# Second feed-forward layer from two 12-bit halves of the gelu in one-pass float32r, with a new table of work places

## Time and profile before

| | |
|---|---|
| median of 3 runs | 1874.81 us (1872.44 to 1875.64) |
| span of the profiled execution | 1875.9 us |
| its own time | not listed apart from the runs; the median lies 1.1 us under the span |
| TensorE clock granted, mean | 0.967 |
| PE busy | 94% of the span |
| DVE busy | 75% |
| ACT busy | 63% |
| POOL busy | 54% |

### The profile page before, as it was taken

One profiled execution on the slowest core, in us unless ns is written; L12 is line 12 of the kernel. 1 busy time (PEld: TensorE's weight loads), 2 busy tenths in 40 slices (PEclk: granted clock), 3 DMA queues, 4 the chain that ended last, 5 costly groups with the idle time before them and its releaser, 6 DMA issues.

```text
span 1875.9 us, 74519 instructions
## 1 busy us (share of the span) xinstructions
PE 1757.2 (94%) x29935; PEld 1283.4 (68%) x29935; DVE 1413.3 (75%) x2997; ACT 1173.6 (63%) x2795; POOL 1020.8 (54%) x3192
## 2 busy tenths in 40 slices
PE   6879899999999999999999999999999999999875
PEld 4545567777777777777777777777777777777653
DVE  4656767787778877787778877787778777787454
ACT  3445666666666666666666666666666666666521
POOL 2102245666566666666566666666566656666632
PEclk8889999999999999999999999999999999999965
DMA  8511111111111111111111111111111111111000
GB/s 228 162 30 37 38 45 40 42 47 48 45 43 43 51 45 45 39 50 45 45 43 46 50 45 42 42 51 45 45 41 48 48 45 45 41 48 29 20 22 21
DMA packets 140912, 92.94 MB, mean 50 GB/s; under 512 B 20196, under 2 KB 139800, under 8 KB 140568
## 3 DMA queue, kind: packets, MB, share of 16 engines
q1 hardware_dynamic: 136368, 87.91, 17.2%
q10 hardware_dynamic: 4200, 0.27, 0.2%
HBM read 31.50 MB, written 18.35 MB: 27 GB/s over the span
## 4 chain that ended last, share of the span: by engine, by line
PE 57%; DVE 19%; SPq 7%; issue 6%; DMA 4%; POOL 3%; ACT 3%; DVEq 0%; ACTq 0%; POOLq 0%
PE gen_bank L766 10%; PE gen_bank L868 9%; PE value_bank L729 8%; DVE nmax L1121 8%; PE score_bank L697 7%; PE max_banks L559 6%; SPq L414 5%; DMA lowstage<-qpiece 3%; PE gate_bank L761 2%; DVE stats L1242 2%; DVE qaug L1137 2%; PE gen_bank L581 2%; PE gen_bank L807 2%; PE gen_bank L776 2%; SPq L417 2%
## 5 line engine op out<-in xcount | busy, mean ns | idle before, releaser
L1068 ACT ACTIVATE probs<-score_bank 128x512 f32<-128x512 f32 x1024 | 604.2, 600 | 238.8 <-PE score_bank L697 226.0
L1121 DVE TENSOR_REDUCE nmax<-max_banks 128x2 f32<-128x1024 f32 x512 | 622.6, 1216 | 89.5 <-PE max_banks L561 85.5
L697 PE MATMUL score_bank<-qaug,kaug 98*128 98x512 bf16 x1024 | 370.9, 387 | 2.4 <-ACT probs L1068 1.4
L729 PE MATMUL value_bank<-probs,vaug 128*32 128x128 f32 x8192 | 332.6, 280 | 0.0
L729 PEld LDWEIGHTS value_bank<-probs,vaug 128*32 128x32 f32 x8192 | 193.9, 109 | 123.2 <-issue 93.6
L1656 POOL TENSOR_TENSOR diff<-gates 128x16 f32<-128x16 f32 x472 | 126.3, 267 | 235.1 <-ACT gates L1074 233.8
L766 PE MATMUL gen_bank<-w2T,hT 128*128 128x256 f32 x1024 | 252.1, 389 | 0.0
L559 PE MATMUL max_banks<-kaug,qaug 64*128 64x512 bf16 x512 | 199.9, 390 | 37.4 <-DVE nmax L1121 35.1
L766 PEld LDWEIGHTS gen_bank<-w2T,hT 128*128 128x128 f32 x1024 | 184.3, 190 | 33.7 <-issue 13.8
L561 PE MATMUL max_banks<-kaug,qlow 64*128 64x512 bf16 x512 | 200.8, 392 | 0.0
L868 PE MATMUL gen_bank<-x1piece,w1Tb 128*128 128x128 bf16 x3072 | 195.2, 220 | 0.5 <-DVE x1rest L1396 0.5
(11 more groups left out here) (233 smaller groups left out, 2968.2 us busy)
## 6 DMA issues: line engine op xcount, KB each, us to landing
qstage<-qpiece SPq DMA_DIRECT2D x384, 64.0 KB
lowstage<-qpiece SPq DMA_DIRECT2D x192, 64.0 KB
xt<-in_L_attn_x SPq DMA_DIRECT2D x64, 128.0 KB
xk<-in_L_attn_x SPq DMA_DIRECT2D x16, 512.0 KB, 7.4
residual<-x2s SPq DMA_DIRECT2D x64, 128.0 KB
x2f<-residual SPq DMA_DIRECT2D x64, 128.0 KB
out<-x SPq DMA_DIRECT2D x64, 128.0 KB
raw<-in_L_ffn_W SPq DMA_DIRECT2D x2, 1024.0 KB, 8.3
```

Of the source, the lines that this page charges most:

```text
L697: pe.matmul(score_bank[t % 2][:, :], kaug[0:AUG, r, tt, u, :], qaug[:, r, u, :, :].rearrange("p h s -> p (h s)"), start=True, stop=True).t ...
L729: last = pe.matmul(value_bank[32 * g:32 * g + 32, :].rearrange("p (k t) -> p k t", k=HG)[:, :, uv * BLOCK_POS:(uv + 1) * BLOCK_POS], vaug[ ...
L1068: act.activation(probs[:, t % 4, :], score_bank[t % 2][:, :], ACT.Exp).then_inc(exp_done, 1)
L1121: dve.tensor_reduce(nmax[:, m % 2, at:at + 3:2], max_banks[:, :, :], AX_X, ALU.max, negate=True).then_inc(max_taken, 1)
```

## The change

`w2T` and two new tiles `hhi` and `hlo` have the type float32r, four bytes that TensorE multiplies in one pass with a shortened mantissa. After the four gelus of a half, ACT copies the half of hT to `hhi` (128x512, rounding it to the short mantissa), and DVE subtracts, `hlo = hT - hhi` (128x512, `low_half`). PE multiplies both by w2T: 16 matmuls per tile in one pass each, where 8 float32 matmuls in several passes were. PE waits for the DVE subtraction (`h_lo`) where it waited for the gelu. The DVE subtractions have places of their own, HLOA=62 and HLOB=65. The three tables of places are new throughout. Tiles are declared in another order, and the buffers of the set-up share their memory with later tiles.

```diff
-PE_AT = dict(XT=22, INPUT=4, Q=0, OUT=27, OT=12, ATT=18, PROJ=29, TURNX=36, B=41, X1T=52, NM=50, FFN1A=56, FFN1B=62, TURND=71, LAST=81, F2_0=63, F2_1=63, F2_2=63, F2_3=63, F2_4=63, F2_5=71, F2_6=71, F2_7=71)
-ACT_AT = dict(XT=21, OT=5, Q=0, ATT=23, Q8=62, TURNX=32, X1T=51, TURND=71, GELUA=59, GELUB=59)
-DVE_AT = dict(Q=2, X2R=8, X3R=28, X2=19, OT=14, X3=56, QUANT=62, XN=26, ORDER=28, LN1=39, X1=46, BS=45, SCAN=60, X1P=51, NM=52, X4R=86, X4=111)
-POOL_AT = dict(LN2=6, LN3=53, PIECES=0, X2S=15, QIN=59, XD=63, X3B=54, LN1=38, X1B=60, LN4=97, LNI=15)
+PE_AT = dict(XT=23, INPUT=1, Q=3, OUT=25, OT=13, ATT=19, PROJ=27, TURNX=35, B=45, X1T=51, NM=48, FFN1A=58, FFN1B=61, TURND=75, LAST=80, F2_0=63, F2_1=64, F2_2=66, F2_3=66, F2_4=69, F2_5=70, F2_6=74, F2_7=74)
+ACT_AT = dict(XT=19, OT=3, Q=0, ATT=23, Q8=63, TURNX=32, X1T=50, TURND=76, GELUA=56, GELUB=57)
+DVE_AT = dict(Q=2, X2R=9, X3R=24, X2=15, OT=11, X3=58, QUANT=62, XN=28, ORDER=28, LN1=32, X1=49, BS=44, SCAN=60, X1P=55, NM=50, X4R=87, X4=110, HLOA=62, HLOB=65)
+POOL_AT = dict(LN2=6, LN3=53, PIECES=0, X2S=15, QIN=59, XD=63, X3B=61, LN1=38, X1B=58, LN4=94, LNI=15)
...
-        w2T = sb("w2T", [P, FT, D])
+        w2T = sb("w2T", [P, FT, D], F32R)
...
+        hhi = sb("hhi", [P, FT, P], F32R)
+        hlo = sb("hlo", [P, FT, P], F32R)
...
             def second_layer(f):
-                return pe.matmul(gen_bank[0][:, 0:D], hT[:, f, :], w2T[:, f, :], start=(f == 0), stop=(f == FT - 1), skip_group_check=True)
+                pe.matmul(gen_bank[0][:, 0:D], hhi[:, f, :], w2T[:, f, :], start=(f == 0), stop=False, skip_group_check=True)
+                return pe.matmul(gen_bank[0][:, 0:D], hlo[:, f, :], w2T[:, f, :], start=False, stop=(f == FT - 1), skip_group_check=True)
...
                             if f == 0:
                                 wait(pe, emptied[0], use(0, "F2_0", m))
+                                pe.wait_ge(h_lo, 2 * m + 1)
                             if f == FT // 2:
-                                pe.wait_ge(emptied[1], use(1, "FFN1B", m) + 1)
+                                pe.wait_ge(h_lo, 2 * m + 2)
...
                                 last.then_inc(emptied[half], 1)
+                                act.wait_ge(emptied[half], use(half, name, m) + 1)
+                                rows_of = slice(4 * half, 4 * half + 4)
+                                act.activation(hhi[:, rows_of, :], hT[:, rows_of, :], ACT.Copy).then_inc(h_hi, 1)
...
+            def low_half(m, half):
+
+                dve.wait_ge(h_hi, 2 * m + half + 1)
+                rows_of = slice(4 * half, 4 * half + 4)
+                dve.tensor_tensor(hlo[:, rows_of, :], hT[:, rows_of, :], hhi[:, rows_of, :], ALU.subtract).then_inc(h_lo, 1)
```

More of the change, by code:

```diff
@@ L12 @@
 BF16 = mybir.dt.bfloat16
+F32R = mybir.dt.float32r
 FP8 = mybir.dt.float8e4
@@ L183, in block_net, with setup_sb @@
         probs = sb("probs", [P, 4, 512])
+        hT = sb("hT", [P, FT, P])
+        csum = sb("csum", [P, R, GROUP, BLOCK_POS])
+        go_on = sb("go_on", [P, GROUP, BLOCK_POS])
+        states = sb("states", [P, 2, BLOCK_POS, B])
+        hseq = sb("hseq", [P, 2, STEPS, B])
+        qscale = sb("qscale", [P, 3, D // QBLOCK])
+        square = sb("square", [P, 1])
+        stats = sb("stats", [P, 5, 6])
+        meanvar = sb("meanvar", [P, 5, 2])
+        veps = sb("veps", [P, 5])
+        rstd = sb("rstd", [P, 5])
+        LN1, LN2, LNI, LN3, LN4 = range(5)
+        setup_memory = ExitStack()
+        def setup_sb(name, shape, dt=F32):
+            return setup_memory.enter_context(nc.sbuf_tensor(name, shape, dt))
+        raw_q = setup_sb("raw_q", [P, KT, D])
+        raw_kv = setup_sb("raw_kv", [DK, 2, D])
+        raw_o = setup_sb("raw_o", [P, KT, D])
+        raw_1 = setup_sb("raw_1", [P, FT, D])
+        raw_2 = setup_sb("raw_2", [P, KT, F])
+        raw_b = setup_sb("raw_b", [P, D])
+        raw_c = setup_sb("raw_c", [P, KT, N])
+        raw_g = setup_sb("raw_g", [P, 4, D + P])
+        raw_ow = setup_sb("raw_ow", [P, KT, P])
+        raw_f = setup_sb("raw_f", [P, KT, D])
+        tern = probs[:, :, :].rearrange("p a b -> p (a b)")
+        fq = setup_sb("fq", [P, KT * D], FP8)
+        fs = setup_sb("fs", [P, 3, KT * D // QBLOCK])
+        xk = setup_sb("xk", [P, XK, TT, D])
+        xTk = setup_sb("xTk", [P, 2, KT, S])
+        kpiece = setup_sb("kpiece", [P, 3, S], BF16)
+        kvT = hT[:, FT // 2:FT, :].rearrange("p f t -> p (f t)")
+        kres = hT[:, 0:FT // 2, :].rearrange("p f t -> p (f t)")
+        setup_memory.close()
+        hhi = sb("hhi", [P, FT, P], F32R)
+        hlo = sb("hlo", [P, FT, P], F32R)
         oT = sb("oT", [P, HG, P])
@@ L192, in block_net @@
         x1rest = sb("x1rest", [P, KT, P])
-        hT = sb("hT", [P, FT, P])
         x2r = sb("x2r", [P, D])
@@ L198, in block_net @@
         xnT = sb("xnT", [P, KT, P])
-        xdT = sb("xdT", [P, KT, P])
         bs = sb("bs", [P, GROUP, BLOCK_POS])
-        csum = sb("csum", [P, R, GROUP, BLOCK_POS])
-        go_on = sb("go_on", [P, GROUP, BLOCK_POS])
-        states = sb("states", [P, 2, BLOCK_POS, B])
         gates = sb("gates", [P, GW])
@@ L207, in block_net @@
         mixed = sb("mixed", [P, B])
-        hseq = sb("hseq", [P, 2, STEPS, B])
         x2f = sb("x2f", [P, D])
@@ L212, in block_net @@
         x3b = sb("x3b", [P, D])
-        qscale = sb("qscale", [P, 3, D // QBLOCK])
         qin = sb("qin", [P, D])
@@ L218, in block_net @@
         x4 = sb("x4", [P, D])
[L219 to L244, removed]
+        xdT = sb("xdT", [P, KT, P])
         k_dram = nc.dram_tensor("key_pieces", [R, TT, 2 * DK, 3 * S], BF16, kind="Internal").ap()
@@ L308, in block_net @@
         x2f_loaded = sem("x2f_loaded")
+        h_hi = sem("h_hi")
+        h_lo = sem("h_lo")
         ssm_step = sem("ssm_step")
@@ L883, in _ @@
                 if s == TAIL_SSM["F2"]:
-                    pe.wait_ge(emptied[1], use(1, "FFN1B", TILES - 1) + 1)
                     pe.wait_ge(emptied[0], use(0, "F2_0", TILES - 1))
+                    pe.wait_ge(h_lo, 2 * TILES)
                     for f in range(FT):
@@ L1402, in work @@
                             dve.tensor_tensor(x1piece[:, 2, :, :], x1rest[:, :, :], x1piece[:, 1, :, :], ALU.subtract).then_inc(x1_step, 1)
+                        for half, name in enumerate(("HLOA", "HLOB")):
+                            m = mine(name, "FFN")
+                            if m is not None:
+                                low_half(m, half)
                         m = mine("NM", "MAX")
@@ L1418, in _ @@
             run_times(dve, tile_time)
+            for half, name in enumerate(("HLOA", "HLOB")):
+                if DVE_AT[name] >= SLOTS:
+                    low_half(TILES - 1, half)
             for s in range(TAIL_STEPS + 3 * STEPS):
```

## The result

| | before | changed |
|---|---|---|
| median | 1875.22 us (4 runs) | 2171.4 us (4 runs, 2166.27 to 2174.22) |
| span of the profiled execution | 1875.9 us | 2172.5 us |
| mean clock granted | 0.967 | 0.919 |

The ratio is 1.158, with a 95% interval of 1.156 to 1.160: 16% slower. The forecast was 2100 us with a range from 1995 to 2200, so the sign held and the range holds the result, but 2171 lies 71 us above the forecast and outside the band of the main case, 2050 to 2150.

What follows compares the result with a forecast made beforehand. PE and a closed loop of five legs through all engines were taken as two bounds of about equal height. Loop growth of 3.75 us a tile gave 210 + 8 + 4 = +222 us: 2098, rounded to 2100 us, range 1995 to 2200.

Steps and rivals of the forecast that it cites:

- main case: The summed legs hold, with a loop between 29.4 and 31.1 us a tile: 2050 to 2150 us, chance 0.62.
- Leg A: From DVE's rest of the queries (line 1125) through nine transfers to ORDER: forecast unchanged at 11.13 us.
- Leg B: DVE from ORDER to the end of X1, now behind tick 12's reduction: 6.7 us instead of 5.09.
- leg C: From X1 to the end of the exponential of tick 14: forecast unchanged at 2.86 us.
- Leg D: ACT through the gelus to the tanh of step 7, adding two copies, losing FFN1B's wait: 7.0 us instead of 6.63.
- Leg E: From the tanh to the next line 1125, with INPUT and two second-layer pairs now before Q: 3.1 us instead of 1.10.
- upper bound of 0.221: Time in us of one new second-layer matmul if its weight load isn't hidden or the format takes two passes; 0.11 taken.
- the prediction's last rival: The format doesn't run in one pass: 3.5 us more PE work, 0.4 more in Leg E, 2125 us; inside the main case.
- F2_0's wait: PE's wait for the first low half: costs nothing while the tanh is later, under a microsecond if not.
- The discount for quick transfers: Tiles with a quicker transfer don't wait for the landing, so the loop's mean was lowered from 30.8 to 30.2 us.
- The clock: Rival: PE's clock falls in thinner stretches; a third of the time at 1.2 GHz adds 1.3 us a tile, 2175 us; chance 0.13.
- The rival that PE was the only bound: The loop stays under PE, so 1.77 us less second layer a tile gains 113 us: about 1763 us, chance 0.12.

Runs made afterwards that it cites:

- e1: The changed kernel with 24 spare bfloat16 matmuls of 128 columns, result unused, ahead of every INPUT: 2105.67 us.
- e2: The changed kernel's new places with the old arithmetic (8 float32 matmuls, no copy to a high half, no subtraction): 2074.0 us.
- e3: The new arithmetic on the four tables of places of the kernel before, with the subtractions at DVE slots 62 and 63: 1921.61 us.
- e4: The changed kernel with INPUT back at PE slot 4 and Q back at slot 0, nothing else: 1993.53 us.
- e5: The changed kernel with X1 moved back from DVE slot 49 to 46 (tick 11), nothing else: 2076.27 us.
- e6: The changed kernel with INPUT at 4, Q at 0 and X1 at 46: 1908.72 us.
- e7: Old places with the new one-pass halves, FFN1B at 61, gelus at 56 and 57, and copies, subtractions and second layer moved later: 1876.11 us.
- e8: The kernel before, float32 second layer, with FFN1B alone moved from PE slot 62 to 61: 1865.32 us.
- e9: e7 with the first half's copy at ACT slot 56, its subtraction at DVE 61 and F2_0 to F2_3 at PE slot 63: 1867.34 us.

## Why the prediction was right, and by how much it was short

The mean legs of all tiles that start between 600 and 1500 us, taken from the timelines as for the one tile above, with the granted clock of that stretch:

| | A | B | C | D | E | sum | clock |
|---|---|---|---|---|---|---|---|
| before | 10.76 | 5.10 | 2.86 | 6.63 | 1.10 | 26.45 | 1.00 |
| changed | 10.87 | 6.63 | 2.90 | 6.82 | 4.28 | 31.49 | 0.94 |
| e1, hole filled | 10.73 | 6.63 | 3.18 | 6.88 | 2.95 | 30.36 | 0.98 |
| e2, old arithmetic | 11.24 | 6.63 | 2.94 | 5.60 | 3.34 | 29.76 | 0.99 |
| e3, old places | 10.74 | 5.09 | 2.86 | 7.30 | 1.10 | 27.08 | 1.00 |
| e4, Q first | 10.83 | 6.63 | 2.89 | 6.85 | 1.10 | 28.30 | 0.99 |
| e5, X1 early | 10.75 | 5.41 | 2.80 | 6.82 | 4.00 | 29.78 | 0.96 |
| e6, both | 10.85 | 5.41 | 2.80 | 6.82 | 1.10 | 26.98 | 1.00 |
| e7, copies late | 11.92 | 5.09 | 2.86 | 5.49 | 1.10 | 26.47 | 1.00 |
| e8, before, FFN1B at 61 | 11.16 | 5.09 | 2.86 | 5.49 | 1.77 | 26.37 | 1.00 |
| e9, copy A early | 11.10 | 5.10 | 2.86 | 6.15 | 1.11 | 26.31 | 1.00 |

- **What bounds the kernel.** Right: PE and the loop, at about one height. e8 shows the PE side (64 us of waiting on the loop removed, 11 us gained), e4 and e5 the loop side (178 and 95 us, for 1.86 and 1.22 us of legs, and the clock).
- **The matmuls.** One pass, as taken (0.11). The chain of waits in e7, at the full clock, columns start, length and what:

```profile
1003.97 0.12 PE gen_bank L778
1004.09 0.12 PE gen_bank L777
1004.21 0.12 PE gen_bank L778
```

  The halves stand 0.12 us apart. The upper bound of 0.221, and with it the reading of weight load and matmul in series, is out: the weight loads are recorded with 187 to 194 ns on average in e3 and e7, and yet the matmuls follow at 0.12. By the Trainium skill, TensorE: Matmul & The Clock Gate, section LDWEIGHTS, a load of 128 columns takes 128/1.2, or 107 ns. The recorded length of the loads is longer than that; the pace of 0.12 leaves room for 107 ns where the load runs beside the matmul before. One slip stands in the prediction's last rival: at 0.221 a half, PE would have 1.8 us more work than with one pass and as much as before, not 3.5 more; its time of 2125 us came from leg E and doesn't hang on it.
- **Leg D**, forecast 7.0, measured 6.81: the copy takes 0.63, the second gelus overlap its end. **Leg E**, 3.1 against 2.96 at the full clock (its 0.04 from Q to ACT, which the rows cited with it don't hold, is 0.04 here: 1035.99 to 1036.03). **Leg B**, 6.7 against 6.62. **Leg A** and **C** unchanged, as said.
- **F2_0's wait** cost the legs nothing, as said, since ACT is the later one in that stretch: the holes are 0.76 us for the low half and 1.93 for the tanh. But it isn't free of consequence, see the clock.
- **The discount for quick transfers** was right in kind and too large. I lowered the loop from 30.8 to a mean of 30.2. Leg A means 10.87 us, where the tile above has 11.08, so the discount was worth 0.2 to 0.3 and not 0.6; the legs' terms were together 0.5 too long. With leg E at its full-clock 2.95 and leg C at 2.80 the means would sum to 30.07, near the forecast mean because the two errors cancel. That is luck.
- **The clock** is the step that failed. The sum has no term for it; I put it among the rivals with 0.13 and +1.3 us a tile, 2175 us, because my rows didn't show that holes under 2 us were enough. Here they were: behind the hole of 1.9 us, which follows one of 0.5 to 0.8 by about 1 us, the clock falls in 24 of 28 tiles, and INPUT, two pairs and Q run wholly or in part at half of it. This cost 1.33 us a tile in leg E and 0.10 in leg C. The rival's 2175 against 2171 is partly luck: its 1.3 us was a third of the time at the low level for 4 us of PE work all round the loop, where in truth 2.4 us of work in one leg is hit nearly always. With this fall taken away (e1, which has others, worth about 0.3 us a tile) the kernel takes 2105.67 us, against my 2100 for the case without any.
- **Which hole does it** is only in part shown. At INPUT and behind it the clock falls where two long holes stand close together: 0.76 and 1.93 us in the changed kernel (24 of 28 tiles), 1.14 and 1.51 in e5 (21 of 30). It doesn't fall there where the second is short (0.75 and 0.58 in half the tiles of e1, 0.76 and 0.38 in e4) or where there is one alone, be it 1.02 us (e2) or 1.68 (e3). No run has the 1.9 alone.
- **The rival that PE was the only bound** (1763 us) fell twice: e3 at 1922, and e8.

## What to carry to other kernels

Where one engine is busy 94% and still holds only 57% of the chain, close the loop: add up the legs from one piece of work to its own next turn, and compare the sum with the period. A change is worth what it takes off that sum, and a piece that is put behind a late semaphore costs all that stands between it and the loop's next leg.

In a hand-made order, a faster operation that needs a conversion first can arrive later than the slow one did. In e7 its saving became a hole where the old matmuls had covered a wait.

Price a hole on TensorE twice, once as time and once as clock for what stands behind it, and look for a second hole close by.

Compare a new version with the best old one. e9 looked 0.3% faster than the kernel before, and one of its numbers alone, moved in the old kernel, gave 0.5%.

## What the runs showed of the hardware that I had not expected

- A hole on PE of about 1.9 us with a short one before it was followed by a granted clock of 0.50 in 24 of 28 tiles; a hole of 1.68 us without a second one (e3) was not, in any tile between 600 and 1500 us. Filling it with 24 unused matmuls brought the clock from 0.94 to 0.98 and made the kernel 3% faster (2171 to 2106 us). TensorE: Matmul & The Clock Gate of the Trainium skill, section on the HAM clock gate, says that activity releases the throttle, and this agrees in direction; by its advice on idle gaps (section "Why this matters for your kernels"), whose limit is longer than any hole here, a hole of 1.9 us would have been harmless, and there the measurement decides.
- A DVE subtraction with both inputs in SBUF slows POOL while it runs. POOL's cast of a 128x256 tile takes 398 ns in the kernel before and 811 on average in e7, where it runs beside the subtraction, and the product that divides by the scales (POOL, 128x256) takes 619 ns before and 955 in the changed kernel, where it does. In each kernel the other of the two, which has no subtraction beside it, keeps its time (the cast 396 ns in the changed kernel, the product 617 in e7). The Trainium skill, SBUF — State Buffer, section "SBUF: two separate sides", says that DVE and GpSimd share one pair of ports as an exclusive lock, and that a DVE operation with two SBUF inputs holds it against one of GpSimd that reads SBUF, for the whole instruction; the trace agrees: in e9 the cast that started 0.11 us after the subtraction took 0.84 us, about its own 0.40 and most of the 0.58 that the subtraction still had to run. Groups of instructions by line (busy us, mean ns, idle us and its releasers), kernel before and e7 in this order:

```profile
L1501 POOL CAST qpiece<-qrest 128x256 bf16<-128x256 f32 x64 | 25.4, 398 | 130.6 <-DVE qrest L1125 130.6
```

```profile
L1539 POOL CAST qpiece<-qrest 128x256 bf16<-128x256 f32 x64 | 51.9, 811 | 118.7 <-DVE qrest L1150 112.8 <-issue 0.4
```
